# First norm of blocks 2 and 3 from the input laid out by feature, second norms placed later

## What is computed

```python
x = L0_attn_x
x = x + _L0_attn_ref(_layernorm(x, axis=-1), ...)
...
h = _layer_norm(x, ln1_g, ln1_b)
hh = _time_shift(h)
k = (h * tm_mk + hh * (1 - tm_mk)) @ Wk.T
v = (h * tm_mv + hh * (1 - tm_mv)) @ Wv.T
r = (h * tm_mr + hh * (1 - tm_mr)) @ Wr.T
wkv = _wkv_run(k, v, tm_first, tm_decay)
x = x + jax.nn.sigmoid(r) * wkv @ Wo.T
h = _layer_norm(x, ln2_g, ln2_b)
```

## Time and profile before

| | |
|---|---|
| median of 3 runs | 1055.93 us (1055.35 to 1056.35) |
| the profiled execution's own time | 1056.01 us |
| its span, first to last instruction | 1054.2 us |
| PE busy | 1046.7 us, 99% |
| DVE busy | 695.7 us, 66% |
| POOL busy | 604.7 us, 57% |
| ACT busy | 516.2 us, 49% |
| PE in the chain that ended last | 96% |

### The profile page before, as it was taken

How to read it: one execution, slowest core, us unless ns; L and a number is a source line. 1 busy time by engine, 2 the same in 40 slices (tenths; PEclk the granted TensorE clock), 3 DMA queues, 4 the chain that set the end, 5 groups by cost and what they waited for, 6 DMA issues and landing times.

```text
span 1054.2 us, 13559 instructions
## 1 busy us (share of the span) xinstructions
PE 1046.7 (99%) x4712; PEld 866.6 (82%) x4712; DVE 695.7 (66%) x1215; ACT 516.2 (49%) x873; POOL 604.7 (57%) x500
## 2 busy tenths in 40 slices
PE   8999999999999999999999999999999999999999
PEld 7788888788888888888888888888888888888887
DVE  7888756786545565465449656767698566666655
ACT  7867676757444354333345433343345244444442
POOL 7776373725665654444537755668664366555552
PEclk9999999999999999999999999999999999999999
DMA  9002042267644344643333665575446445444432
GB/s 323 1 1 41 1 108 78 95 198 276 254 152 157 122 169 129 211 153 117 92 108 110 227 216 199 186 250 198 146 175 219 145 147 188 151 160 160 156 105 80
DMA packets 46212, 158.27 MB, mean 150 GB/s; under 512 B 4672, under 2 KB 5056, under 8 KB 41536
## 3 DMA queue, kind: packets, MB, share of 16 engines
q1 hardware_dynamic: 30688, 109.07, 29.9%
q0 software_dynamic: 15168, 48.24, 15.2%
q10 hardware_dynamic: 288, 0.09, 0.0%
HBM read 98.65 MB, written 58.73 MB: 149 GB/s over the span
## 4 chain that ended last, share of the span: by engine, by line
PE 96%; POOL 2%; DVE 1%; ACT 0%; DMA 0%; issue 0%; DVEq 0%; ACTq 0%
PE bank L611 14%; PE bank L612 14%; PE bank L613 14%; PE bank L600 14%; PE bank L602 14%; PE bank L601 14%; PE bank L787 2%; PE bank L788 2%; PE bank L789 2%; PE bank L675 1%; PE bank L778 1%; PE bank L681 1%; POOL weights L1920 0%; POOL operand L1932 0%; POOL weights L1932 0%; PE bank L833 0%
## 5 line engine op out<-in xcount | busy, mean ns | idle before, releaser
L611 PE MATMUL bank<-combo,left 128*128 128x512 f32 x672 | 262.1, 390 | 0.4 <-DVE bank L1666 0.4
L613 PE MATMUL bank<-combo,left 128*128 128x512 f32 x672 | 261.5, 389 | 0.0
L612 PE MATMUL bank<-combo,left 128*128 128x512 f32 x672 | 261.4, 389 | 0.0
L1597 DVE TENSOR_TENSOR resid<-bank,resid 128x512 f32<-128x512 f32 x176 | 120.4, 688 | 130.6 <-PE bank L602 129.8
L1995 POOL TENSOR_TENSOR inner<-made,inner 128x512 fp32r<-128x512 f32 x96 | 127.6, 1350 | 116.5 <-ACT inner L1099 116.4
L1955 POOL TENSOR_TENSOR left<-quart,left 128x512 fp32r<-128x512 f32 x96 | 115.1, 1221 | 84.9 <-ACT left L1062 44.7
L600 PE MATMUL bank<-right,inner 128*128 128x512 f32 x384 | 149.6, 390 | 0.0
L602 PE MATMUL bank<-right,inner 128*128 128x512 f32 x384 | 149.4, 389 | 0.0
L601 PE MATMUL bank<-right,inner 128*128 128x512 f32 x384 | 149.4, 389 | 0.0
L611 PEld LDWEIGHTS bank<-combo,left 128*128 128x128 f32 x672 | 126.2, 188 | 27.5 <-DVE bank L1666 1.1
L613 PEld LDWEIGHTS bank<-combo,left 128*128 128x128 f32 x672 | 126.2, 188 | 26.2
(11 more groups left out here) (193 smaller groups left out, 1947.6 us busy)
## 6 DMA issues: line engine op xcount, KB each, us to landing
kept_left<-left SPq DMA_DIRECT2D x24, 1792.0 KB, 8.2
left<-kept_left POOLq DMA_DIRECT2D x24, 1024.0 KB, 7.0
left<-kept_left POOLq DMA_DIRECT2D x24, 768.0 KB, 5.0
quart<-wide SPq DMA_DIRECT2D x24, 512.0 KB, 4.2
tall_staged<-tall SPq DMA_DIRECT2D x48, 256.0 KB, 5.1
raw<-kept SPq DMA_DIRECT2D x32, 256.0 KB, 6.1
landed<-wts SPq DMA_DIRECT2D x20, 256.0 KB, 5.9
resid<-x POOLq DMA_DIRECT2D x4, 1024.0 KB, 9.6
```

The costliest lines, as they stand in the source:

```text
L611: pe.matmul(acc[:], hi, combo[:, c, k, 0, :], start=fresh and k == 0, stop=False, skip_group_check=True)
L612: pe.matmul(acc[:], hi, combo[:, c, k, 1, :], start=False, stop=False, skip_group_check=True)
L613: mm = pe.matmul(acc[:], lo, combo[:, c, k, 0, :], start=False, stop=k == 1, skip_group_check=True)
L1597: dve.tensor_tensor(tile, A[s][:], tile, ALU.add).then_inc(added, 1)
```

## The change

Blocks 2 and 3 of the first norm no longer go through TensorE. A second copy of the input, laid out by feature on the host (`x_feat`), is loaded into `held[:, 0]` and `held[:, 1]`. VectorE still takes the statistics by token. It copies means and reciprocals into `row_stats` (`norm1_rows`), SP sends them through `rows` and back into `extra` on all partitions (`keep_rows`, `load_rows`), POOL takes the means off (`norm1_centred`) and VectorE multiplies by the scales straight into the banks `A` (`norm1_scaled`), between the pieces of `wkv_weight`. The normed tiles by token, which `output` and the residual need, are written one block later. The second norm's statistics of a block go behind mix r of the next, its tiles behind the gated value; the DMA that adds x goes with them.

```diff
             def norm1_stats(b, moments_there=False):
-                dve.wait_ge(x_loaded[b - 1], 16)
+                dve.wait_ge(x_loaded[b - 1], 32 if b >= PAIRS else 16)
...
+            def norm1_rows(b):
+                dve.wait_ge(ln_rstd, nth_norm(1, b))
+                dve.wait_ge(rows_moved, rows_until(b - PAIRS))
+                dve.tensor_copy(row_stats[:, 0, :], stats1[:, b, :, 0]).then_inc(rows_moved, 1)
+                dve.tensor_copy(row_stats[:, 1, :], rstd1[:, b, 1, :]).then_inc(rows_moved, 1)
+
+            def norm1_scaled(b, tiles):
+                dve.wait_ge(rows_moved, rows_until(b - PAIRS + 1))
+                for k in tiles:
+                    dve.wait_ge(centred, KT * (b - PAIRS) + k + 1)
+                    tile, bank_of = (t.rearrange("q (s p) -> q s p", s=SUBS) for t in (held[:, b - PAIRS, k, :], A[k][:]))
+                    scale = extra[:, 1, :].rearrange("q (p s) -> q s p", s=SUBS)
+                    dve.tensor_tensor(bank_of, tile, scale, ALU.mult).then_inc(t1_psum, 1)
...
+            def norm1_centred(b):
+                pool.wait_ge(x_loaded[b - 1], 32)
+                pool.wait_ge(rows_moved, rows_until(b - PAIRS + 1))
+                for k in range(KT):
+                    tile = held[:, b - PAIRS, k, :].rearrange("q (s p) -> q s p", s=SUBS)
+                    mean = extra[:, 0, :].rearrange("q (p s) -> q s p", s=SUBS)
+                    pool.tensor_tensor(tile, tile, mean, ALU.subtract).then_inc(centred, 1)
...
@@ SP, before the loads of ITEM_CR @@
+                sp.dma_start(held[:, b - PAIRS], x_feat[b - PAIRS]).then_inc(x_loaded[b - 1], 16)
+            for n in range(FIRST_BY_FEATURE):
+                keep_rows(n)
+                load_rows(n)
...
@@ TensorE, loop @@
                 key(b)
-                if b + 1 < BLOCKS:
-                    norm1(b + 1)
-                else:
+                if b + 1 == BLOCKS:
                     norm2(0)
                 value(b)
...
@@ VectorE, loop @@
+                else:
+                    norm2(b - 2)
                 if b + 1 < BLOCKS:
                     norm1_stats(b + 1)
                 mix("k", b)
+                if b + 1 < BLOCKS:
+                    norm1_rows(b + 1)
+                if b >= PAIRS:
+                    norm1(b)
+                    back_to_first(b)
                 mix("v", b)
                 output(b - 1)
                 if b + 1 < BLOCKS:
-                    norm1(b + 1)
-                    back_to_first(b + 1)
                     last_token(0, b)
-                norm2_stats(b - 1)
-                wkv_weight(b)
-                norm2(b - 1)
-                if b + 1 < BLOCKS:
+                    wkv_weight(b, range(2))
+                    norm1_scaled(b + 1, range(1))
+                    wkv_weight(b, range(2, 3))
+                    norm1_scaled(b + 1, range(1, 2))
+                    wkv_weight(b, range(3, KT))
+                    norm1_scaled(b + 1, range(2, KT))
                     mix("r", b + 1)
+                    norm2_stats(b - 1)
+                else:
+                    norm2_stats(b - 1)
+                    wkv_weight(b)
+                    norm2(b - 1)
...
@@ POOL, loop @@
                 operand_lo("y", b - 1)
+                if b >= PAIRS:
+                    x_added(b - 2)
                 if b + 1 < BLOCKS:
                     norm1(b + 1)
                 operand_lo("k", b)
                 operand_lo("v", b)
+                if b + 1 < BLOCKS:
+                    norm1_centred(b + 1)
+                    operand_lo("r", b + 1)
                 norm(nth_norm(2, b - 1))
-                if b + 1 < BLOCKS:
-                    operand_lo("r", b + 1)
-                x_added(b - 1)
+            x_added(BLOCKS - 2)
```

More of the change, by code:

```diff
@@ L226, with rows_until @@
 CACHED = tuple(u for u in range(UNITS) if not is_fresh(u))
+FIRST_BY_FEATURE = BLOCKS - PAIRS
+def rows_until(n):
+    return 34 * min(n, FIRST_BY_FEATURE) + 32 * max(n - FIRST_BY_FEATURE, 0)
 def nth_norm(which, b):
@@ L235, with build @@
 MIXES = {"r": 0, "k": 1, "v": 2, "cr": 3, "ck": 4}
-def build(nc, x, wts, wide, tall, down, vectors, identity, out):
+def build(nc, x, x_feat, wts, wide, tall, down, vectors, identity, out):
     x_blocks = x.rearrange("o (b s p) h -> (o b) p s h", p=P, s=SUBS)
@@ L329, in build @@
         kept_raw = nc.dram_tensor("kept_raw", (2, P, KT, BT), F32, kind="Internal").ap()
-        rows = nc.dram_tensor("rows", (PAIRS, 2, BT), F32, kind="Internal").ap()
+        rows = nc.dram_tensor("rows", (BLOCKS, 2, BT), F32, kind="Internal").ap()
         kept_left = nc.dram_tensor("kept_left", (KEY_UNITS + GATE_UNITS, P, 2, SEVEN, HALF), F32,
@@ L1632, in norm3_rows @@
                 dve.wait_ge(t3_kept, SUBS * (j + 1))
-                dve.wait_ge(rows_moved, 32 * (j - PAIRS + 1))
+                dve.wait_ge(rows_moved, rows_until(j + 1))
                 tile, plain, mean, scale = rows_of(j, k)
-                dve.tensor_tensor(tile, plain, mean, ALU.subtract).then_inc(z3_part, 1)
-                dve.wait_ge(z3_part, KT * (j - PAIRS) + k + 1)
+                dve.tensor_tensor(tile, plain, mean, ALU.subtract).then_inc(centred, 1)
+                dve.wait_ge(centred, KT * j + k + 1)
                 dve.tensor_tensor(tile, tile, scale, ALU.mult).then_inc(z3_ready, 1)
@@ L1970, in norm3_rows @@
                 pool.wait_ge(x2_made, SUBS * (j + 1))
-                pool.wait_ge(rows_moved, 32 * (j - PAIRS + 1))
+                pool.wait_ge(rows_moved, rows_until(j + 1))
                 tile, plain, mean, scale = rows_of(j, k)
-                pool.tensor_tensor(tile, plain, mean, ALU.subtract).then_inc(z3_part, 1)
-                pool.wait_ge(z3_part, KT * (j - PAIRS) + k + 1)
+                pool.tensor_tensor(tile, plain, mean, ALU.subtract).then_inc(centred, 1)
+                pool.wait_ge(centred, KT * j + k + 1)
                 pool.tensor_tensor(tile, tile, scale, ALU.mult).then_inc(z3_ready, 1)
@@ L2154 @@
         "x": np.ascontiguousarray(take("attn_x")),
+        "x_feat": np.ascontiguousarray(take("attn_x")[0, PAIRS * BT:].reshape(PAIRS, BT, KT, P).transpose(0, 3, 2, 1)),
         "wts": np.ascontiguousarray(np.stack(pieces)),
```

27 lines of the change are left out of this document (17 added, 10 removed).

## The result

The changed kernel takes **1060.95 us** (median; 1059.77 to 1061.69) beside 1055.93 for the kernel before (1055.10 to 1056.35): ratio 1.0047, 95% interval 1.0032 to 1.0062. It is slower. The forecast was 1063.1, the range 1053.5 to 1066.5. The profiled execution took 1061.03, 5.02 more than that of before.

What follows compares the result with a forecast made beforehand. The prediction took TensorE, busy 99% of the span, to bound the kernel. Transposes -3.5, waits +6.5 and +2.3, slow pace +1.9 gave +7.2 on a median of 1055.93: 1063.1 us, range 1053.5 to 1066.5.

Steps and rivals of the forecast that it cites:

- a first wait already at the receptance of block 2: Sign of being wrong: TensorE first waits at the receptance of block 2, near 93 us, which would mean late rows.
- Transposes: Two groups of sixteen transposes leave TensorE, 1.75 us each; a gain of 3.5 us in all.
- Step 1: Block 2's means and reciprocals: VectorE's copies end at 65.5, and after two transfers the rows land at 74.0.
- Rival (4): The rows come later than 74 and lengthen the same wait; at 3 us late 1066 to 1067; chance 0.07.
- Step 2: POOL's four mean subtractions take 6.2 us from 74.0, ending at 81.4 with two turns of VectorE.
- Step 3: VectorE's products and scalings put mix r(2) at 88.3; its low parts reach TensorE in time, no wait, 0.1 to spare.
- Step 4: At output(1), mix k(2) ends at 109.3 and the first gate at 110.5; TensorE asks at 104.0 and waits 6.5 us.
- Step 5: At output(2), the first gate of block 3 ends at 156.3, TensorE asks at 154.0: a 2.3 us wait.
- Step 6: TensorE runs at half pace after the long wait: 1.9 us taken, from 0 to 2.9.
- (1): Rival: the waits come, but no slow pace behind them; 1061.2 us; chance 0.18.
- (2): Rival: VectorE keeps the port for all four second-norm tiles; waits 4.05 and 0, 1056.5 us, slow pace to 1059.4; chance 0.15.
- (3): Rival: the port holds VectorE up at none of these places; TensorE waits 0.9 once, 1053.3 us; chance 0.18.

Runs made afterwards that it cites:

- e12: e10 with the rows of means and scales of blocks 2 and 3 stored in token order, so they are read one element after the other: 1055.09 us.
- e8: e7 with VectorE's first gated value moved ahead of the second norm's statistics: 1054.76 us.
- e4: The changed kernel with POOL held until the second norm's four tiles are done, before the y low parts of blocks 1 and 2: 1059.33 us.
- e2: The changed kernel with the second norm's four tiles moved behind mix k and the row copies, the load of x later too: 1058.12 us.
- e7: The changed kernel with ScalarE's gates of the first two receptance tiles ahead of the operands of k for blocks 2 and 3: 1058.25 us.
- e11: e10 without the move of ScalarE's gates: 1054.39 us.
- e10: e8 with the second norm's four tiles moved behind output(b-1), their load of x last on POOL: 1053.06 us, ratio 0.9977 to the kernel before.
- e3: The changed kernel with the second norm's statistics ahead of the weights of the values and its tiles behind mix k: 1054.81 us.
- e1: The changed kernel with only the second norm's statistics back ahead of the weights of the values: 1061.76 us.

## Why the prediction was right, and where not

The sign was right, and the sum was near: slower, +7.2 forecast, +5.0 measured. The mechanism at output(1) was right: ScalarE's gate behind a late mix k(2), half pace behind the wait, the tiles in turns with POOL. But that wait was less than half of the one forecast, 3.5 us were lost where none was forecast, and the wait forecast for block 3 did not come; that the sum was near is in good part luck. One of the prediction's own signs of being wrong, a first wait already at the receptance of block 2, came true, though not for the reason given there, late rows. Term by term:

**Transposes**, -3.5: measured -1.79 and -1.80.

**Step 1**, rows at 74.0. The copies ended at 65.00 (65.5 forecast), but the rows landed sooner than the 4.5 us taken from the third norm. Copies, then SP's queue:

```profile
62.56 1.19 DVE L1454 COPY row_stats<-stats 128x4 f32<-128x4 f32 x1
63.66 1.34 DVE L1455 COPY row_stats<-rstd 128x4 f32<-128x4 f32 x1
```

```profile
65.03 0.38 SPq L528 DMA_DIRECT2D rows<-row_stats  x1
66.61 0.33 SPq L537 DMA_DIRECT2D extra<-rows  x1
```

SP sends the second when the first has landed, 1.6 us. Rival (4) never came near; POOL started the means at 72.70, when its own low parts were done.

**Step 2**, means off by 81.4: done at 79.21, three of them at 1.54. By the Trainium skill (GPSIMD Engine Reference, section 7, Performance pitfalls for Q7 kernels) the stride would have cost about half as much again; e12 measures it, 1.54 against 1.28, a fifth.

**Step 3**, mix r(2) at 88.3: it was 86.97, still early, since means and scalings were. "TensorE asks for the first at 93.1 and for the last at 95.1. No wait" is **the step that failed**. It looked at the operand alone. The matmul needs its bank too, and the value product in it is taken by the gated value, which the change put behind 3.5 us of statistics. The text even had the gated value at 95.0, later than the 93.1 at which TensorE asks, and did not put the two side by side. It cost 1.9 and 1.5 us. e8 shows it: with the first gated value ahead of the statistics both losses are gone.

**Step 4**, 6.5 at output(1): 2.9. The gate ended at 108.2 instead of 110.5: 1.3 from step 3, some 0.4 from a power of 1.01 instead of 1.39, the rest from the tiles. And TensorE asked at 105.3 instead of 104.0, as it had already lost 1.9 at receptance(2). The turns were sized well (up to 1.52 a tile, end at 100.96).

**Step 5**, 2.3 at output(2): none. The gate ended at 156.16 and the matmul started at 156.26. What block 3 lost (1.5) was again the bank of the receptance, another mechanism, so this step failed too.

**Step 6**, 1.9 of slow pace: 3.0. The clock line settles what it could not before: 0.50 in the windows from 108 to 114. The rule cited from the Trainium skill (TensorE: Matmul & The Clock Gate, What's actually happening) by which the array then gets half of its pulses agrees with that row.

The rivals: (1) falls with the clock line, though its 1061.2 is the number nearest to the measured one; (2) and (3) fall with the tiles in turns (e4 shows what they take without). Forecast less measured, the errors are 3.6 (step 4), 2.3 (step 5), -1.1 (step 6), -3.5 (step 3) and 0.1 (transposes), 1.4 together; the other 0.8 is this execution's.

Open: why some executions of e2, e7 and e8 lose 2 to 3 us more than others. A likely reason is the first row copy. Where it is long, mix r(2) starts some 1.5 us later, and in e4 that was enough for a wait of 2.31 at receptance(2) and half clock behind it. The profiled executions of e2 (1055.0) and e8 (1053.79), with the short copy, lie below the medians of their kernels, that of e11 (1056.27), with the long one, above its median, and that of e12 (1055.07), also with the long one, in the upper of its two groups. No kernel was profiled with both lengths, so this is not shown, nor is what decides between them.

## What to carry to other kernels

When work is taken off the bounding engine, it comes sooner everywhere behind: list for each of its next products every release it needs (operand, bank, gate), with the time of each, and not only the one that was last before. A helper engine that sits idle with its input ready and another engine's late result ahead in its list is the cheapest thing to mend: two gates moved past four waiting operands took away the 5.9 us lost at output(1). The median came down from 5.0 to 2.8 us above that of before only, since the next wait grew, so one must take away all the waits on the path: e7, e8 and e10 each exposed the next. And before two traces are compared for a cause, look whether they already differ ahead of the edit, as the row copy did here.

## What the runs showed of the hardware

A wait can cost more than its length. In the profiled executions twelve waits of TensorE of 1.15 (e3) to 1.78 us (e4) left the granted clock at 1.00. With waits of 2.29 (e7), 2.31 (e4) and 4.89 (e1) it went to 0.50 for 3.4 us, which cost a further 1.7 to 1.8 us; with 2.73 (the changed kernel) it went to 0.50 for 6.8 us, of which the last 6 cost a further 3.0. No wait between 1.78 and 2.29 was seen, and the one at the start of the span (3.9 us, granted clock 1.00) is not counted.

Beside dense POOL work a VectorE instruction from SBUF to SBUF often lasts until POOL's is over: tiles 0.54 alone, up to 1.52 beside POOL's low parts and 1.77 beside its means (e10), a copy of four columns 0.16 alone and 1.19 beside POOL. In five of the eleven traces that have it, that copy outlasted four of POOL's instructions in a row (4.94 to 4.96). So a tiny instruction can cost more than a tile. The statistics' reads (0.67 to 0.69) and the products with a bank as input (0.67 to 0.69) kept their length beside the same POOL work.

A two-input fp32 operation with one operand read in steps of four elements took 1.07 on VectorE and 1.54 on POOL, with all in order 0.69 and 1.28.
